# A four-layer transformer on one core: four moves of work between engines and between stages

## The reference

```python
x = x + L0_attn(norm(x))   # 16 heads of 8; scores of later blocks of 32 keys are set to 0, not masked
x = x + L0_ffn(norm(x))    # fp4: x, h and the weights rounded to a grid, in blocks of 16 with a scale
x = x + L1_attn(norm(x))   # LoRA projections, ALiBi, causal
x = x + L1_ffn(norm(x))    # ternary: silu(x w1) * (x w2), then gelu(. h1), gelu(. h2), . w3
x = x + L2_attn(norm(x))   # full attention: softmax(q k / sqrt(8)) v
x = x + L2_ffn(norm(x))    # rwkv: sigmoid(xr Wr) * (relu(xk Wk)^2 Wv), xr, xk mix each token with the one before
x = x + L3_attn(norm(x))   # state-space block: conv of 4 taps, decayed scan, coupling, output norm
x = x + L3_ffn(norm(x))    # 8 experts, two branches, cumulative sums, a router
```

## Time and profile before

| | us |
|---|---|
| median of 3 runs (lowest, highest) | 2034.86 (2034.24, 2039.74) |
| the profiled execution, its own time | 2043.07 |
| its span in the profile | 2041.2 |
| L0 attention, about | 0 to 407 |
| fp4, about | 407 to 573 |
| ternary | 916 to 1239.8 |
| L2 attention | 1239.8 to 1628.6 |
| tail | 1628.6 to 2041.2 |

### The profile page before, as it was taken

How to read it: one execution, slowest core, us unless ns; L and a number is a source line. 1 busy time by engine, 2 the same in 40 slices (tenths; PEclk the granted TensorE clock), 3 DMA queues, 4 the chain that set the end, 5 groups by cost and what they waited for, 6 DMA issues and landing times.

```text
span 2041.2 us, 33165 instructions
## 1 busy us (share of the span) xinstructions
PE 1800.4 (88%) x11885; PEld 810.0 (40%) x11885; DVE 1316.3 (64%) x3506; ACT 1041.5 (51%) x1768; POOL 608.3 (30%) x701
## 2 busy tenths in 40 slices
PE   4888888856679999999999999999999868999998
PEld 1233333334434445444554452332333234444443
DVE  3778788599857787751011016998999437667663
ACT  1566666612126666664223222887888734544432
POOL 4244354255422332211011011222322046444420
PEclk9999999977769999999999997999999969999999
DMA  6354222000132234200000022322222010000000
GB/s 133 100 139 98 63 63 63 4 15 0 44 81 64 64 91 98 64 2 2 0 1 0 0 62 60 66 64 64 63 63 63 11 43 0 6 6 6 6 11 11
DMA packets 67964, 91.69 MB, mean 45 GB/s; under 512 B 10924, under 2 KB 61340, under 8 KB 62924
## 3 DMA queue, kind: packets, MB, share of 16 engines
q1 hardware_dynamic: 66072, 89.04, 18.2%
q10 hardware_dynamic: 1728, 0.53, 0.1%
HBM read 49.30 MB, written 39.85 MB: 44 GB/s over the span
## 4 chain that ended last, share of the span: by engine, by line
PE 53%; issue 5%; DVE 4%; ACT 3%; DMA 2%; SPq 1%; POOL 1%; DVEq 0%; POOLq 0%; ACTq 0%
PE ps L1556 5%; PE ps L412 5%; PE ps L1568 5%; PE ps L386 4%; PE ps L2979 3%; PE ps L1448 3%; PE ps L2247 3%; PE ps L398 3%; PE ps L2265 2%; PE ps L2249 2%; PE ps L370 2%; PE ps L332 2%; DMA Qst<-mT 2%; PE ps L354 1%; PE ps L1940 1%
## 5 line engine op out<-in xcount | busy, mean ns | idle before, releaser
L702 DVE TENSOR_REDUCE mx<-ps 128x1 f32<-128x512 f32 (+3 forms) x1024 | 534.0, 581 | 100.9 <-PE ps L354 70.8
L600 ACT ACTIVATE Pr<-ps 128x1024 f32<-128x1024 f32 (+3 forms) x512 | 347.7, 707 | 178.8 <-PE ps L337 96.7
L593 ACT ACTIVATE Pr<-ps 128x512 f32<-128x512 f32 x512 | 275.4, 602 | 46.0 <-PE ps L386 39.2
L354 PE MATMUL ps<-Kst,Qst 63*128 63x512 bf16 (+3 forms) x1024 | 222.6, 315 | 55.1 <-DVE mx L702 29.7
L698 DVE CUSTOM_DVE_ANT_0 vs<-ps,cT 128x512 f32<-128x512 f32 (+3 forms) x512 | 225.7, 487 | 63.4 <-PE ps L354 60.1
L332 PE MATMUL ps<-Qst,Kst 64*128 64x512 bf16 (+3 forms) x1024 | 221.8, 309 | 20.3 <-ACT Pr L600 8.5
L370 PE MATMUL ps<-Pr,V 128*32 128x512 f32 (+3 forms) x2048 | 196.2, 455 | 6.6 <-ACT ctxU L606 3.1
L3007 POOL TENSOR_TENSOR ve<-mv,eps 128x4 f32<-128x4 f32 x41 | 8.3, 202 | 584.9 <-DVE mv L2996 584.9
L398 PE MATMUL ps<-Kst,Qst 63*128 63x512 bf16 x512 | 172.9, 404 | 5.6 <-DVE mx L702 3.3
L412 PE MATMUL ps<-Pr,V 128*32 128x256 f32 x2048 | 164.5, 393 | 8.7 <-ACT ctxU L606 7.8
L386 PE MATMUL ps<-Qst,Kst 64*128 64x512 bf16 x512 | 157.8, 388 | 10.6 <-DMA Qst<-mT 6.5
(11 more groups left out here) (339 smaller groups left out, 3253.2 us busy)
## 6 DMA issues: line engine op xcount, KB each, us to landing
Qst<-parts_scratch SPq DMA_DIRECT2D x48, 384.0 KB, 6.3
Kst<-parts_scratch SPq DMA_DIRECT2D x48, 384.0 KB, 8.4
parts_scratch<-qpart SPq DMA_DIRECT2D x24, 384.0 KB, 2.7
parts_scratch<-kpart SPq DMA_DIRECT2D x24, 384.0 KB, 3.2
parts_scratch<-qpart SPq DMA_DIRECT2D x24, 256.0 KB, 2.9
parts_scratch<-kpart SPq DMA_DIRECT2D x24, 256.0 KB, 3.3
parts_scratch<-qpart SPq DMA_DIRECT2D x24, 128.0 KB, 2.8
parts_scratch<-kpart SPq DMA_DIRECT2D x24, 128.0 KB, 3.2
```

Source lines behind the costliest of these rows:

```text
L354: mm = pe.matmul(ps[:, 4 + a, lo:lo + W], k.Qst[rows, n.par, pair, P * it:P * it + P], k.Kst[rows, n.par, pair, 0:W], start=True, stop=True)
L593: act.activation(k.Pr[:, g % 2, 2 * (j // 2) + 1 - j % 2, :], ps[:, self.bank_t(b, g, j), :], ACT.Exp).then_inc(self.s_exp.sem, 1)
L600: act.activation(k.Pr[:, g % 2, 2 * tile:2 * tile + 2, 0:W], ps[:, 2 * tile:2 * tile + 2, 0:W], ACT.Exp).then_inc(self.s_exp.sem, 1)
L702: dve.tensor_reduce(k.mx[:, half, at:at + 1], ps[:, bank, lo:lo + W], AX_X, ALU.max, negate=True).then_inc(self.s_max.sem, 1)
```

## The change

Four edits in one version.

1. **Tail work in L2's last frame.** `Tail` becomes the guest of the full attention. The tail's frame -3 is gone; its steps (rwkv of batch 0 with its constants, the statistics and norms of batch 1 for rwkv and of batch 0 for the state-space block, the two constants) are issued in slots 0 to 8 of frame 8. The sigmoid of batch 0 is made as exp(-x) on ACT, then add 1 and reciprocal on VectorE. The late weights are loaded from SP once batch 6 of L2 is done, into the half of the memory that belongs to even batches; two of their temporaries move to `qpart`. GpSimd's wait for all late weights moves to the tail's frame -1.
2. **fp4.** VectorE makes the scale of x ahead of the gated product. GpSimd waits, before it divides h, until VectorE has done the first two of the four rounding instructions of x, and before it multiplies x back, until VectorE has done the first two for h.
3. **Block reciprocals on GpSimd.** The denominator's add and its inverse move from VectorE to GpSimd, as a power of -1, for all quarters but quarters 1 to 3 of the last batch.
4. **Batch 0's first 32 maxima of L2.** Their score matmuls are issued by PE between the last 14 products with h2 of ternary's last batch, two or three after each, into banks 2 and 3; VectorE reduces them there.

```diff
+    def early_scores(self, pe, u):
...
+        if u == 0:
+            pe.wait_ge(self.s_stacked.sem, self.s_stacked.at(n))
+        pe.wait_ge(self.s_max.sem, self.s_max.at(n, at - 1))
+        pe.matmul(k.ps[:, self.bank_m(n, at), :], k.Qst[rows, 0, pair, P * it:P * it + P],
+                  k.Kst[rows, 0, pair, :], start=True, stop=True).then_inc(self.s_scores.sem, 1)
...
-                if self.kind == "block" and s in (2, 6, 10) and prev.valid():
+                if self.kind == "block" and s in (2, 6, 10) and prev.c == NB - 1:
                     inverse(prev, 1 + s // 4)
-                if self.kind == "block" and s == 14 and f.valid():
-                    inverse(f, 0)
...
+            if q == 0 or b.c < NB - 1:
+                den = k.cT[:, q % 2, :].rearrange("p (t a c) -> p t a c", t=NT, a=4)[:, :, :, DH]
+                pool.tensor_tensor(k.dn2[:, :, :], k.dn[:, half, :, 4 * w:4 * w + 4], den, ALU.add)\
+                    .then_inc(self.s_inverse.sem, 1)
+                pool.wait_ge(self.s_inverse.sem, self.s_inverse.at(b, 2 * q + 1))
+                pool.tensor_tensor(k.rec[:, :, :], k.dn2[:, :, :],
+                                   k.mone[:, 0:1].unsqueeze(2).broadcast_to([P, NT, 4]), ALU.pow)\
+                    .then_inc(self.s_inverse.sem, 1)
...
+            if later.valid() and f.valid():
+                quantize(self.q_x, later, 0)
             if f.valid() and nxt.valid():
                 gated(nxt)
...
                 self.q_x.gpsimd(pool, later, 0)
+                pool.wait_ge(self.q_x.s_magic.sem, self.q_x.s_magic.at(later))
...
             if later.valid() and f.valid():
+                pool.wait_ge(self.q_h.s_magic.sem, self.q_h.s_magic.at(f))
                 self.q_x.gpsimd(pool, later, 1, self.s_xnT_ps)
...
+        def quota(products):
+
+            return max(0, (products - 2) * 32 // 14)
...
+                if f.c == NB - 1:
+                    done += 1
+                    if done == 3:
+                        pe.wait_ge(self.s_a.sem, self.s_a.at(f))
+                    for u in range(quota(done - 1), quota(done)):
+                        after.early_scores(pe, u)
...
         ahead(dve, frame)
+        for u in range(32):
+            self.after.early_maximum(dve, u)
         add(N(None, NB - 1))
...
+    def dve_inverse(self, dve, n):
+        dve.wait_ge(self.s_denominator.sem, self.s_denominator.at(n, 1))
+        dve.tensor_scalar(self.r, self.r, 1.0, None, ALU.add).then_inc(self.s_denominator.sem, 1)
+        dve.wait_ge(self.s_denominator.sem, self.s_denominator.at(n, 2))
+        dve.reciprocal(self.r, self.r).then_inc(self.s_r.sem, 1)
...
+    def early_tensor(self, pe, f, s):
+        if f.c != NB:
+            return
+        r, zero = self.rwkv, N(None, 0)
+        if s == 0:
+            pe.wait_ge(self.before.s_max.sem, self.before.s_max.at(f.plus(-1)))
+            r.pe_turn(pe, zero)
+        elif s == 2:
+            r.pe_keys(pe, zero)
+        elif s == 3:
+            r.pe_receptance(pe, zero)
+        elif s == 6:
+            r.pe_values(pe, zero)
+        elif s == 7:
+            self.ssm.pe_constants(pe, self.k.ps[:, 4, :])
...
                 if st.stage == max(FIRST_STAGE, FIRST_LATE):
-                    k.stage_starts(sp, st)
+                    attention, n = st.before, N(None, NB - 2)
+                    sp.wait_ge(attention.s_scores.sem, attention.s_scores.at(n))
+                    sp.wait_ge(attention.s_scores_t.sem, attention.s_scores_t.at(n))
+                    sp.wait_ge(attention.s_pv.sem, attention.s_pv.at(n))
                     k.load_late(sp, st.ssm.loads)
```

More of the change, by code:

```diff
@@ L2392, with __init__ @@
 class Tail(Stage):
-    def __init__(self, k, stage, fp4, ternary):
-        self.fp4, self.ternary = fp4, ternary
+    def __init__(self, k, stage, fp4, ternary, before):
+        self.fp4, self.ternary, self.before = fp4, ternary, before
         super().__init__(k, stage)
@@ L2423, in tensor, with frame @@
         last = e.STEPS - 1
-        def frame(f, opening, folding):
+        def frame(f, folding):
             before, en, sn, rn = f.plus(-1), f.plus(1), f.plus(2), f.plus(3)
@@ L2482, in frame @@
                         s.pe_out(pe, sn)
-            if opening:
-                s.pe_constants(pe)
+        pe.wait_ge(s.s_couple, 1)
         self.frames(frame)
@@ L2696, in make_stages @@
     fp4.after, ternary.after = l1, l2
+    tail = Tail(k, 5, fp4, ternary, l2)
     l0.guest, fp4.before = fp4, l0
+    l2.guest = tail
     l1.guest, ternary.before = ternary, l1
-    return [l0, fp4, l1, ternary, l2, Tail(k, 5, fp4, ternary)]
+    return [l0, fp4, l1, ternary, l2, tail]
 def layout(inp):
@@ L2883, in late @@
         size = int(np.prod(shape[1:])) * mybir.dt.size(dt) // 4
-        r = next(r for r in range(3) if self.late_at[r] + size <= self.late_mem[r].shape[1])
+        order = (3, 4, 5, 0, 1, 2) if src is None else (0, 1, 2)
+        r = next(r for r in order if self.late_at[r] + size <= self.late_mem[r].shape[1])
         at = self.late_at[r]
```

137 lines of the change are left out of this document (104 added, 33 removed).

## The result

The change takes 2014.34 us (median of 4 runs, 2010.94 to 2022.73) against 2035.36 of the kernel before beside it (2034.24 to 2039.74): a ratio of 0.9894, 95% interval 0.9872 to 0.9915, 17 to 26 us faster. The forecast was 2005.4 with a range of 1992 to 2019: the direction and the range hold, the gain was put 8 to 9 us too high.

A forecast was written before the change was run, and what follows sets the result against it. No single engine bounds the whole: PE, VectorE or ACT by stage, nobody full at the L2-tail seam. Terms -21.5 - 7 + 6 - 7 = -29.5 from the median 2034.86 gave 2005.4 us, range 1992 to 2019.

The forecast's parts named there:

- Part 1: Seam from L2 to the tail: the tail's opening of 26.8 us goes, less the guest's costs; term -21.5 us.
- The late loads: End of L2: loads issued early in frame 8 should be over before 1633; if not, the term is -17.
- the context: L2's last frame: ACT's added work makes the last context come some 2 to 3 us later.
- Part 2: Ternary to L2: 32 early maxima lengthen ternary but bring L2's first exponential score earlier; term -7 us, between -9.5 and -5.
- the length of the 14 rounds: Ternary's last h2 products: rounds of about 1.45 or 2.05 us with early scores, stage end 9.7 us later.
- the keys: Start of L2: batch 1's keys land at 1272.7, stage end 1249.5; PE waits some 2 us in slot 14.
- Part 3: fp4: the new order and waits move GpSimd's division onto other VectorE instructions; term +6 us, from -9 to +9.
- The sum for a frame: One fp4 frame: -3.5 + 1.35 + 2.0 to 2.6 + 1.05, so +0.9 to +1.5 us, in six frames.
- Part 4: L0: the block reciprocals' add and inverse leave VectorE for GpSimd; term -7 us, from -9.7 to +22.
- 9.7 us at most, if all of it is arrears on PE like the 0.38: L0: VectorE loses 0.25 and 0.2 us 22 times; the most gained if PE waited for all of it.
- The price of the power: L0: GpSimd's power of 16 columns, bounds 1.02 to 4.1 us, taken as 2.3 with no stall.
- the stall's threshold of 3.0: L0: room for 9.1 us of powers; above 3.0 us each, each of seven frames stalls 3X - 9.1.

The follow-up runs named there:

- f_order: The change with both new GpSimd waits in fp4 taken out and its VectorE order kept: 2008.18 us, 0.9849 of the kernel before.
- f_hfirst: The change with fp4's VectorE order and waits as before, and GpSimd dividing h ahead of x: 2007.33 us, 0.9854 of the kernel before.
- p_double: The change with a second GpSimd power of 16 columns ahead of each block reciprocal's power: 2071.97 us in a single execution.
- u_inv: The change with the block reciprocals put back on VectorE: 2020.61 us, 0.9916 of the kernel before.
- p_add: The change with GpSimd's power of 16 columns turned into an add, leaving the reciprocal out: 2012.76 us, 0.9875 of the kernel before.

## Why the forecast came out as it did

**Part 1: -21.5 forecast, -19.9 in the profile, -19.1 by undoing it.** The mechanism and its terms held: the opening of 26.8 went (26.5 by the table, -1.7 to -28.2), and the last add came later by 6.6 where 5.2 were set. The reciprocal took 3.35, forecast 3.3. What hung over the last context was what the prediction named, the norm's end and the shift: 1624.0 to 1625.66, 1.6 us more than before and a little under the 2 to 3 that were set. The late loads were in time. The mis-sized term is the context: it came 5.0 later (40.3 us behind L2's seventh add, 35.3 before) where 2 to 3 were set. ACT's added work and its longer waits for PE stand in that stretch (0.73 and 0.98 between exponentials, where the earlier trace rows has 0.39); no run splits the 5.0 between the two.

**Part 2: -7 forecast, -5.4 in the profile, -6.3 by undoing it.** The mis-sized term is the length of the 14 rounds: 12.4 us added, 9.7 forecast. Both engines' pieces came out longer. A pair of products between scores takes 1.06 us from its start to the next (1231.30 to 1232.36), and 0.86 in a row of eight (four pairs from 1217.05 to 1220.48); ten such pairs are 2 us. VectorE's 32 maxima took 20.9 us in nine rows in place of 19.2, since one that starts anew takes 0.69 and not 0.60 as in a row of 37. And the two engines took turns: VectorE waited 8.3 us for PE and PE's weight loads 14.5 for VectorE. No run splits the 2.7 us that were missing between them. The rest came as worked out: the first score for an exponential 4.2 behind the stage's end (4.6), the keys 23.0 behind it (23.2), a wait of 1.4 in slot 14 (2).

**Part 3: +6 forecast, +4.2 to +5.4 in the profile, +3.3 by undoing it.** The sign and the cause were right: 1.28 for xn (1.35), 2.27 in line 1101 of x (2.0 to 2.6), 0.73 in line 1101 of h (1.05). The sum for a frame was too dark, +0.9 to +1.5 against +0.26, by one row that wasn't looked at: before, line 1051 of h stood beside the multiplication of x and took 0.5 more than its own time (0.88 now), and that relief wasn't booked. And a cost wasn't seen: x is multiplied back 3.8 us later in its frame (17.8 us behind line 3133, 14.0 behind the same step before), so PE has it later, and in the frame after the last x, which has no rounding of x to cover it, VectorE waits for PE's gate products. So the part's cost is 0.26 in each of five frames and 3.7 in that one, and not about 1 in each of six. Two errors of opposite sign made a good total, and that was luck; the runs without the waits tell them apart.

The Trainium skill's rule on the shared port pair (SBUF — State Buffer, section "Who interferes with whom") agrees with every fp4 run here: in four orders the division's 2.6 us fell on a VectorE instruction that by this rule can take the pair, a `tensor_scalar` (2.79 before, 2.38 in f_order) or one with two SBUF inputs (2.96 in the change, 1.54 in f_hfirst), and not on the gated products, which read PSUM: beside f_hfirst's division two of them took 0.94, as without it.

**Part 4: -7 forecast, -1 to -2 in the profile.** This is the step that failed: "9.7 us at most, if all of it is arrears on PE like the 0.38". The price of the power was guessed at 2.3 and is 2.9; that it stayed under the stall's threshold of 3.0 was luck, by 0.1 us. The threshold itself held (the 0.1 us ahead of PE's turn, and p_double). But VectorE's saved 0.45 in 22 slots wasn't arrears. PE's waits in L0 for the maxima, by the line of the scores (us, times), in before and in the change:

```profile
  DVE mx L702: 29.7, 79
```
```profile
  DVE mx L734: 28.5, 81
```

They fell by 1.2 us, and by 0.6 to 3.1 if all profiles with and without part 4 are compared (26.6 to 28.5 against 29.7 and, in u_inv, 29.1). At least part of what VectorE no longer did became idle time of its own, behind PE's scores (of the same two views, who waited for these scores, us and times, in before and in the change):

```profile
  DVE mx L702: 70.8, 64
```
```profile
  DVE mx L734: 79.6, 76
```

(76.1 in u_inv, and 78.6 to 81.1 in the nine profiles with part 4.) The row of 0.38 was one narrow slot, taken as a sign for all 22. Why the rest of PE's waits stays isn't shown by a run; p_add, whose powers are 2.7 us shorter, leaves 26.3. Undoing the part by runs gave 4.5 with some 6 of doubt, so the forecast 7 can't be excluded from the medians alone; the frames in the profiles say 1 to 2.

The sum of the terms was -29.5, the two profiles differ by 23.4 in the stretches touched: 5 of the missing 6 are part 4, and the errors of the three others partly cancel (+1.6, +1.6, -1.8). The 2.4 from there to the medians' 21.0 are within their interval.

## What to carry to other kernels

A wait that keeps GpSimd off one VectorE instruction doesn't remove the collision, it moves it to the next one: look for VectorE work that keeps its time beside a GpSimd pass (here the products that read PSUM and the reduction; a `tensor_scalar` with one input did not), and put the pass beside that, here by swapping two GpSimd instructions (4.5 us in the profile). To price work taken off an engine that isn't the bound, read the sum of the waits for it over the whole stage before multiplying one wait by a count. Work filled into another engine's stretch in small pieces costs more than in a row, on both engines: 1.06 in place of 0.86 a pair of products, 0.69 in place of 0.60 a maximum.
